# Postponing the tree stage of a two-layer recurrent block behind four attentions

## The reference

```python
xn = _layernorm(x)
s = _L0_attn_ref(xn, Wq, Wk, Wv, Wpost)        # 16 heads, 4 groups, softmax over 512 keys
g = _silu(_L0_ffn_ref(xn, ...))                # 64 experts, 8 per token, 256 slots each
x = x + s * g                                  # "x1" in the kernel
xn = _layernorm(x)                             # "xn1"
s = _L1_attn_ref(xn, ...)                      # convolution, then a state scan over 512 tokens
g = _silu(_L1_ffn_ref(xn, ...))                # 8 binary decision trees, depth 7, as matmuls
x = x + s * g                                  # the output
```

## Time and profile before

| | us |
|---|---|
| median of 3 runs | 2681.95 (2681.63 to 2683.68) |
| the profiled execution | 2662.33, of it 2660.2 in the span |
| PE busy | 2227.6 (84%) |
| DVE busy | 1854.1 (70%) |
| ACT busy | 1771.1 (67%) |
| POOL busy | 1738.2 (65%) |

### The profile page before, as it was taken

One profiled execution on the slowest core, in us unless ns is written; L12 is line 12 of the kernel. 1 busy time (PEld: TensorE's weight loads), 2 busy tenths in 40 slices (PEclk: granted clock), 3 DMA queues, 4 the chain that ended last, 5 costly groups with the idle time before them and its releaser, 6 DMA issues.

```text
span 2660.2 us, 38038 instructions
## 1 busy us (share of the span) xinstructions
PE 2227.6 (84%) x13155; PEld 1413.0 (53%) x13192; DVE 1854.1 (70%) x2832; ACT 1771.1 (67%) x3282; POOL 1738.2 (65%) x1416
## 2 busy tenths in 40 slices
PE   6776989999698889898989898889888989888761
PEld 4444667775454556455655565456445645554441
DVE  5878554543347876687668767786778666788888
ACT  3556633346278776788677867786778678766862
POOL 1000264416767888887888789887977797665565
PEclk9888999999899999999999999999999999999895
DMA  4000278864555667555765485447534754377776
GB/s 161 25 21 5 83 206 236 240 201 79 95 133 120 119 136 179 117 114 114 174 125 105 94 197 117 94 107 179 117 83 90 185 115 90 87 174 166 176 168 151
DMA packets 282032, 344.50 MB, mean 130 GB/s; under 512 B 66159, under 2 KB 211504, under 8 KB 281840
## 3 DMA queue, kind: packets, MB, share of 16 engines
q0 software_dynamic: 84080, 175.67, 35.3%
q1 hardware_dynamic: 175248, 144.83, 18.8%
q10 hardware_dynamic: 22512, 21.57, 2.4%
HBM read 198.26 MB, written 26.80 MB: 85 GB/s over the span
## 4 chain that ended last, share of the span: by engine, by line
POOL 21%; PE 19%; issue 13%; ACT 11%; DVE 8%; DMA 1%; another core or an unknown queue 0%; POOLq 0%; DVEq 0%; ACTq 0%
POOL arena L1667 8%; POOL acc_sb L1645 6%; DVE bank L1542 3%; POOL arena L1673 3%; POOL arena L1683 3%; PE bank L1784 3%; PE bank L1745 2%; PE bank L1801 2%; PE bank L1947 2%; ACT PT L1024 2%; PE bank L1789 2%; PE bank L1916 2%; ACT bank L1167 2%; PE bank L1839 2%; ACT Pr L1055 1%
## 5 line engine op out<-in xcount | busy, mean ns | idle before, releaser
L1667 POOL TENSOR_TENSOR arena<-arena 128x512 f32<-128x512 f32 x512 | 875.5, 1788 | 19.4 <-DVE arena L1533 17.5
L1645 POOL DMA_INDIRECT acc_sb<-ybuf,slot_idx x256 | 423.2, 1653 | 126.0 <-DMA ybuf<-arena 62.4
L1258 DVE TENSOR_REDUCE negmax<-bank 128x1 f32<-128x512 f32 x512 | 328.6, 683 | 212.9 <-PE bank L1784 211.9
L1167 ACT ACTIVATE bank<-arena,A_sb 128x512 f32<-128x512 f32 x512 | 354.3, 696 | 166.5 <-DVE arena L1547 138.4
L1542 DVE TENSOR_TENSOR_SCAN bank<-bank,arena 128x512 f32<-128x512 f32 x320 | 390.0, 1219 | 82.7 <-ACT bank L1167 44.2
L1673 POOL TENSOR_TENSOR arena<-arena 128x512 f32<-128x512 f32 x192 | 297.2, 1548 | 214.7 <-DVE arena L1542 214.6
L1024 ACT COPY PT<-bank 128x512 f32<-128x512 f32 x512 | 297.5, 592 | 202.1 <-PE bank L1789 193.9
L1055 ACT ACTIVATE Pr<-bank,negmax 128x512 f32<-128x512 f32 x512 | 353.5, 701 | 94.9 <-DVE negmax L1258 94.5
L1784 PE MATMUL bank<-Kp,Qp 64*128 64x512 f32 x1024 | 304.5, 659 | 88.4 <-ACT PT L1024 43.7
L1789 PEld LDWEIGHTS bank<-ident,Pr 128*128 128x128 f32 x2048 | 231.9, 146 | 274.8 <-ACT Pr L1055 214.8
L1683 POOL DMA_DIRECT2D arena<-arena x255 | 283.9, 1113 | 114.6 <-DVE arena L1547 114.3
(11 more groups left out here) (215 smaller groups left out, 3707.9 us busy)
## 6 DMA issues: line engine op xcount, KB each, us to landing
arena<-arena POOLq DMA_DIRECT2D x255, 512.0 KB, 5.3
arena<-bc_dram SPq DMA_DIRECT2D x256, 256.0 KB, 3.9
ybuf<-arena ACTq DMA_DIRECT2D x64, 256.0 KB
arena<-in_w_gate SPq DMA_DIRECT2D x64, 128.0 KB, 3.0
arena<-in_w_up SPq DMA_DIRECT2D x64, 128.0 KB, 3.7
arena<-in_w_down SPq DMA_DIRECT2D x64, 128.0 KB, 4.5
arena<-in_X SPq DMA_DIRECT2D x8, 512.0 KB, 8.2
s_sb<-in_X SPq DMA_DIRECT2D x8, 512.0 KB, 6.9
```

Of the source, the lines that this page charges most:

```text
L1167: act.activation(bank[DECAY[g % 2]][:, :], dt_sb[:, size_slot(b, cb), :], ACT.Exp, scale=A_sb[:, cb, n:n + 1]).then_inc(ssm_decay, 1)
L1258: dve.tensor_reduce(negmax[:, m % RING_STAT:m % RING_STAT + 1], bank[m % RING_S_ATT][:, :], AX.X, ALU.max, negate=True).then_inc(att_max, 1)
L1645: pool.indirect_dma_start(acc_sb[:, i, :], None, ybuf, bass.IndirectOffsetOnAxis(ap=slot_idx[:, b * TILES + i, k:k + 1], axis=0), bounds_c ...
L1667: pool.tensor_tensor(st_sb[:, g % RING_S, :], u_sb[:, size_slot(b, cb), :], B_sb[:, load % RING_BC, :], ALU.mult).then_inc(ssm_input, 1)
```

## The change

The trees are moved behind the first four attentions. The order of the filler becomes attention 0 to 3, trees 0, attention 4, trees 1, attention 5, trees 2, attention 6, trees 3, attention 7, trees 4, 5, 6, 7. `LEAD = 4` is the number of attentions ahead. The rates change: 3.2 units in scan 0, 3.45 afterwards, 3.1 once all attentions are through.

Since a tree batch now runs long after its batch was normalised, three things are kept in DRAM: `xn1` (`xn_dram`, every batch), `x1` (`x1_dram`, all but the last batch) and the state layer's result before the gate (`fin_dram`). SP stores the first two in `ssm_in` and the third in `ssm_store`, loads `xn1` back in `tree_input` (into `g1`, or for batches 5 and 6 into `s_sb`), and the other two in `tree_back`, into a part of `AT`. `ssm_fin` keeps only its first operation; the product with `g1` and the sum with `x1` are done by `tree_gate` on DVE, four 128x512 operations, after which SP stores the output. Batch 7 keeps the old path. The scan no longer waits for trees (`fill_until("trees")` and `"begun"` are gone). The input of a later attention is loaded and normalised by `prepare`.

```diff
+LEAD = 4
-FILL_IN_FIRST = 3.5
+FILL_IN_FIRST = 3.2
-FILL_PER_STEP, FILL_PER_LAST = 3.9, 2.4
+FILL_PER_STEP, FILL_PER_LAST = 3.45, 3.1
...
-        if b < 2:
+        if b < LEAD:
             E.att_begin(b)
...
         for n in range(ATT_STEPS + LAG_RAN):
+            if n == INPUT_AT and b >= LEAD - 1:
+                E.tree_input(b - LEAD + 1)
+            if 2 <= b + 1 < LEAD:
+                prepare(b + 1)
             E.att_step(b, n)
...
+        while not back[0]:
+            bring_back()
+            if not back[0]:
+                yield 0
+        if b < NB - 1:
+            E.tree_gate(b)
...
-        for b in range(NB + 2):
+        for b in range(NB + LEAD - 1):
             if b < NB:
+                yield from prepared(b)
                 yield from attention(b)
                 done["attention"] = b + 1
-            if b >= 1 and b - 1 < NB:
-                while done["normed"] < b:
-                    yield 0
...
+            if b >= LEAD - 1:
+                yield from trees(b - LEAD + 1)
+                done["trees"] = b - LEAD + 2
...
         if b >= 1:
-            fill_until("trees", b)
             yield from tail(b - 1)
...
                 fill_until("attention", b + 2)
-                fill_until("begun", b + 1)
...
+            def ssm_in(self, b, cb):
+                if cb:
+                    return
+                w.wait_ge(x1_norm, 2 * (b + 1))
+                sp.dma_start(xn_dram[b].rearrange("(t p) d -> p t d", p=P), xn1[:, :, :]).then_inc(xn_out, 16)
+                if b < NB - 1:
+                    sp.dma_start(x1_dram[b].rearrange("(t p) d -> p t d", p=P), x1[:, b % 2]).then_inc(x1_out[b % 2], 16)
+            def tree_input(self, b):
+                w.wait_ge(xn_out, 16 * (b + 1))
+                if b <= LEAD:
+                    w.wait_ge(tree_gate, 4 * b)
+                else:
+                    w.wait_ge(cmb_gate, 2 * (b + 2))
+                sp.dma_start(tree_from[b], xn_dram[b].rearrange("(t p) d -> p t d", p=P)).then_inc(xn_in, 16)
+            def tree_back(self, b):
+                w.wait_ge(att_postmm, TILES * attended(b))
+                w.wait_ge(tree_gate, 4 * b)
+                w.wait_ge(stored, 16 * b)
+                w.wait_ge(x1_out[b % 2], 16 * (b // 2 + 1))
+                w.wait_ge(fin_out, 16 * (b + 1))
+                sp.dma_start(back_x, x1_dram[b].rearrange("(t p) d -> p t d", p=P)).then_inc(back_in, 16)
+                sp.dma_start(back_fin, fin_dram[b].rearrange("(t p) d -> p t d", p=P)).then_inc(back_in, 16)
+            def tree_gate(self, b):
+                w.wait_ge(tree_gate, 4 * (b + 1))
+                sp.dma_start(out[b].rearrange("(t p) d -> p t d", p=P), back_fin).then_inc(stored, 16)
...
+            def tree_gate(self, b):
+                half = TILES // 2
+                w.wait_ge(back_in, 32 * (b + 1))
+                for j in range(2):
+                    own = slice(j * half, (j + 1) * half)
+                    w.wait_ge(tree_g1, 2 * b + j + 1)
+                    dve.tensor_tensor(whole(back_fin[:, own, :]), whole(back_fin[:, own, :]), whole(g1[:, own, :]), ALU.mult).then_inc(tree_gate, 1)
+                for j in range(2):
+                    own = slice(j * half, (j + 1) * half)
+                    w.wait_ge(tree_gate, 4 * b + j + 1)
+                    dve.tensor_tensor(whole(back_fin[:, own, :]), whole(back_fin[:, own, :]), whole(back_x[:, own, :]), ALU.add).then_inc(tree_gate, 1)
...
+                if b < NB - 1:
+                    dve.scalar_tensor_tensor(fin_sb[:, i, :], o, alpha_sb[:, 0:1], fin_sb[:, i, :], ALU.mult, ALU.add).then_inc(ssm_fin, 1)
+                    return
```

## The result

The changed kernel takes 2692.89 us (median of 7 runs, 2688.35 to 2698.92), the kernel before 2678.67 us beside it. The ratio is 1.0063, with a 95% interval of 1.0044 to 1.0081: **slower by 0.6%**, where 1.4% faster was forecast. The time lies inside the range (2597 to 2705); sign and size were wrong.

What follows compares the result with a forecast made beforehand. PE was taken as crowded by filler in six scans and idle in the last; terms -120 + 2 + 14 + 44 + 10 + 6 + 7 = -37 us gave 2625 profiled, 2645 us as median, range 2597 to 2705.

Steps and rivals of the forecast that it cites:

- Scans 1 to 5: Each of these scans loses 29 units of filler; predicted saving 120 us in all, between 92 and 148.
- I take 24 a scan: Saving per scan in scans 1 to 5, chosen between 18.4 us (POOL holds 24 of 64 steps) and 29.6 us.
- The second rival: Scans 1 to 5 priced by waits between engines working in order; each falls only 10 us, total 2715 us; chance 0.17.
- Scan 6: First 22 steps get 100 units, 24 of them forced at step 22; predicted +14 us, up to +20.
- The end: After the last step 16 units of trees 7 remain and the late gates' cover is gone; +10 us, 5 to 16.
- Scan 7: 64 steps get 199 units at 1.02 us each, 203 us; predicted +44 us, bounds +40 and +82.
- Scan 0: All attention afterwards: first 24 steps 16.5 us longer, other 40 steps 14.4 less; +2 us, from -5 to +10.
- gates, stores and loads: Added transfers cost nothing; waits at DVE's gates and `tree_begin` cost one us for each of seven; +7 us, 0 to 25.
- SP queue rival: Waits on SP's queue hold rows of B and C beyond their lead and stop the scan; +35, 2680 us; chance 0.04.
- the 19 us held on POOL: If each of 28 DVE gates held POOL for its 0.68 us, 19 us more and 2664; left out of the sum.
- Ahead of scan 0: Loading and normalising attention 2, and attention steps beside the first head, lengthen the start; +6 us, from -2 to +15.
- A first L1667 later than 765 us: Sign in the profile: a first step input on POOL after 765 us would say the start was priced wrong.

Runs made afterwards that it cites:

- bare_old_rates: Changed kernel at the old rates 3.5/3.9/2.4 without any of the six DRAM transfers per batch (output not the reference's); ratio 1.006 to the kernel before.
- phase_shift: Changed kernel with 4.6 units in scan 0, 3.9 in scans 1 to 4, 1.9 in scan 5, 2.6 afterwards, moving attention against the head; ratio 1.0171 to before.
- old_order_new_rates: Kernel before, in its old order, at the new rates 3.2/3.45/3.1, its last filler call allowed to find it exhausted; ratio 1.1525 to before.
- no_back: Changed kernel at 3.2/3.55/3.1 without the trips of `x1` and `fin` through DRAM, gates kept (output not the reference's); ratio 0.9974 to before.
- few_gathers_before: Kernel before with 8 of 32 gathers kept for each later batch (sums incomplete); ratio 1.0001 to before.
- before_again: The kernel before, unchanged, profiled once more; ratio 1.000 to before.
- old_rates: Changed kernel (new order) at the old rates 3.5/3.9/2.4; ratio 1.0095 to before.
- rate_355: Changed kernel with 3.55 instead of 3.45 units per step; ratio 0.996 to before.
- after_busy: Changed kernel at its own rates plus matmuls that nobody reads, ahead of PE's waits; ratio 1.0193 to before.
- rate_30_36_busy: Changed kernel at rates 3.0/3.6/3.1 plus matmuls that nobody reads, ahead of PE's waits; ratio 1.0143 to before.
- rate_32_36_busy: Changed kernel at rates 3.2/3.6/3.1 plus matmuls that nobody reads, ahead of PE's waits; ratio 1.0071 to before.

## Why the prediction was wrong, step by step

**Scans 1 to 5 (forecast -120, came -64.3): the failing step** is "I take 24 a scan", priced by units alone. The tally was right: 29 units leave each scan, also by the plan itself (1115 to 969 for the five). But two terms were wrong.
- *The price of a unit.* 24 lay between 18.4, with the steps that POOL holds giving nothing, and 29.6, all units at the mean price of 1.021 us. In the old order the same rates gave 18.0 us a scan (scans 1 and 2), so the low end was the right one, and for its reason: steps 25 to 63 take 140 us with no filler at all. POOL is near its floor in more steps than the 24 that I took, and at 3.6 us each instead of 3.45. Over five scans this is 30 us of the missing 56.
- *The order* was put at nothing. It costs 6.8 us a scan at the old rates and 6.3 at the new ones, some 31 to 34 us over five scans. The loss lies in the first 24 steps, where attention now stands. It is neither in the transfers (bare_old_rates) nor in one unlucky alignment (phase_shift). Why attention costs more there stays open.

Together they are 61 to 64 us where 55.7 were missing, which is as near as single profiles come.

*The clock* runs through both, and how much of them it is isn't settled. PE was at 1.2 GHz for 72 us more in these scans than before; the lower rates alone raised it from 20.5 to 37.5 us in scans 1 and 2, the order alone from 51 to 79 in scans 1 to 5. At the prices found above, 0.36 to 0.66 us for each, the 72 us would be 26 to 48; by the idle steps of old_order_new_rates some of them cost nothing. The Trainium skill, "TensorE: Matmul & The Clock Gate", section "Terms", prices throttled time at the missing share of the clock, here 0.5 us a us, which gives an estimate of 36 us; the prices found lie on both sides of it. The Trainium skill says on the same page, section "Part 1: The HAM clock gate (the "warmup" mystery)", that the throttled state is the default and activity releases it, which would have been the rule to set against this change. The trace agrees: the clock was 1.00 in the stop of old_order_new_rates' scan 5 (PE busy 130.9 of 142.6 us) and 0.57 right behind it (33.0 of 140.5).

**The second rival** (a scan of 238 us or more) is what came true: 241.9 us on average. Its mechanism, waits between engines that work in order, fits as far as it goes: ACT was at 0.75, DVE at 0.76, PE and POOL at 0.87, none full over the scan. What it lacked was the order's own price, which no row of before could give, and POOL's floor in the later steps.

**Scan 6 (+14, came +24.9).** The price was right and the tally wrong. Steps 0 to 21 took 78.5 us for their 76 units, 1.03 each as forecast. Then the scan stops for 30 us, where I had 25 for 24 forced units; the plan has 40. The steps behind took 5 us more than I left them. The cause of the wrong count is one slip: the plan fits 20 units of attention 2 in ahead of scan 0, and my tally had 34. Those 14 units are missing at every due time behind.

**The end (+10, came +24.8).** The same 14 units stand here again: my tally left 16 units of trees 7, the plan leaves about 29. At 24.8 us that is 0.87 us a unit, where I had reckoned 0.63 (10 for 16) with late gates as a cover.

**Scan 7 (+44, came +31.9).** Here filler was cheaper than priced: 161 of L2024's records in it as forecast, PE at 0.92, and the clock went from 0.80 to 0.95. 117 units more cost 0.27 us each. They went into steps that had room; whether the faster clock helped is not shown by a run. "Near 0.97" was close.

**Scan 0 (+2, came -0.9)** and **gates, stores and loads (+7)** were right or dear in sum: no_back and bare_old_rates show no cost of the transfers. The wait that was to show the SP queue rival exists, but is small: all step inputs of after together, and what POOL waited for there (us, times):

```profile
L1772 POOL TENSOR_TENSOR arena<-arena x512: 1257/1843/2915, 765.3 to 2639.7; 128x512 f32<-128x512 f32 x171
  DVE arena L1635: 18.1, 3
  DMA arena<-bc_dram: 9.4, 7
```

The 9.4 us compare with 1.9 us in one wait before. That rival fell. DVE's gates had waited 7.2 us in all for the silu (L1595).

The gates themselves show something that I had taken for equal work. All 28 (L1595, L1599), and one of them beside a step input:

```profile
L1595 DVE TENSOR_TENSOR AT<-AT,g x14: 677/950/3676, 1251.0 to 2609.2; 128x512 f32<-128x512 f32 x14
L1599 DVE TENSOR_TENSOR AT<-AT x14: 677/679/2893, 1252.7 to 2613.4; 128x512 f32<-128x512 f32 x14
```

```profile
1252.68 3.39 DVE L1599 TENSOR_TENSOR AT<-AT 128x512 f32<-128x512 f32 x2
1253.10 1.82 POOL L1772 TENSOR_TENSOR arena<-arena 128x512 f32<-128x512 f32 x1
```

Eighteen take 0.68 or 0.69 us. The ten others take 1.2 to 3.7, and each ends 0.56 us after the end of a step input that ran beside it on POOL. The 28 take 34.5 us instead of 19.0. By the rule of the Trainium skill ("SBUF — State Buffer", section "SBUF: two separate sides") the gates and POOL exclude each other, and the trace agrees. But it is DVE that waited: the eleven step inputs beside gates took 1.85 us on average, the others 1.84. So the 19 us held on POOL, by which the forecast would have been 2664, are not in the trace, and 15.5 us on DVE are. What they cost the scans is not shown, as no run takes the gates out.

**Ahead of scan 0 (+6, came +13.3).** "A first L1667 later than 765 us" was to say that this was priced wrong, and it came at 765.3; it does not say so. few_gathers_before, which is the kernel before up to the gathers of the second batch, begins its first scan at 765.3 us as well. On the chip that before_again ran on, the old order began at 751.2 and 751.0 us (before_again, old_order_new_rates) and the new one at 754.7 and 752.7 (old_rates, rate_355): 2 to 4 us is what the change costs here. The two that began at 765.3 us lose the time where the experts' weights come in, between 312 and 368 us. The window there in before, in few_gathers_before and in after:

```profile
312.00:368.00 56.00, 46.91 (x336) 32.73 (x335) 31.49 (x65) 23.72 (x56) 41.44 (x39) 0.97 0.70 204
```

```profile
312.00:368.00 56.00, 36.62 (x224) 22.91 (x224) 23.02 (x47) 18.14 (x43) 35.53 (x33) 0.79 0.56 159
```

```profile
312.00:368.00 56.00, 41.47 (x239) 26.40 (x236) 23.36 (x48) 18.86 (x44) 35.77 (x33) 0.76 0.55 161
```

So most likely 13 of the 29.7 us between the two profiles aren't the change's; the other 16.4 agree with the ratio of the runs (0.63% of 2679 us is 16.9).

**The forecast as a whole** had 0.72 on faster (its terms add up to 0.71). It was decided by a term of 120 us, taken as units times a price near the mean, with nothing for the order; had its lower end been some 10 us a scan, which the second rival argued, the sign would have been open. That the time lies inside the range is the range's width and not the mechanism: it had been stretched towards that rival.

## What to carry to other kernels

A mean price of filler (stretch by units) holds for the crowding at which it was read. Price a small withdrawal or addition at the margin, from two stretches that differ in it: here a unit was worth 1.02 us on average, 0.63 when 28 were taken from a scan, and next to nothing where another engine's floor was reached. That floor is read from steps with no filler at all, which a kernel that is held up at a due time shows for free. Write the granted clock beside each such price; where engines hand work round in small steps, thinning out TensorE lowered its clock, and this may return part of the gain. After a reordering, count with the planner itself and not by hand what each due time forces and what is left behind the last step, since both are paid nearly in full: 0.1 unit a step turned this change from 0.6% slower to 0.4% faster, 0.15 unit to 1.2% faster.

## What the hardware showed that I had not expected

- TensorE's clock moved with the filler even though PE stayed over 0.86 busy: of scans 1 to 5 it spent 51 us at 1.2 GHz at PE 0.90 and 123 at PE 0.87. Moving one rate in scan 0 by 0.2 unit changed it by 48 us and the later scans by 28.7. Where PE had next to nothing to do, 121 of 140.5 us at 1.2 GHz cost no time.
- More matmuls meant less time at 1.2 GHz: with 35.8 us of them added in after_busy's scans 1 to 5, it fell by 24 us, in rate_30_36_busy by 27, in rate_32_36_busy, which had 68 us of it, by 3.
- A DVE operation of 128x512 with both inputs in SBUF waited for a POOL one beside it: ten of 28 took 1.2 to 3.7 us instead of 0.68, and each ended 0.56 us after POOL's.
- A lone matmul of 128 columns on 64 columns of weights, two at a time, added 0.10 us of PE's busy time each; in the values' product, where two such go to different halves of the output, 4096 took 286.8 us, 0.07 each.
- What lies ahead of the scans is a matter of the chip, or of the session on it: the four kernels of one group begin them at 751 to 755 us, those of three other groups at 762 to 769, whatever their order or rates (the three with added matmuls, which also stand ahead of the scans, at 779 to 783), with the clock between 312 and 368 us at 0.97 in one (before) and at 0.79 in another (few_gathers_before).
